# Logits of gathered tree rows on VectorE: sixteen multiply-and-sum instructions per tile in place of one multiply, one reduction and one addition

## The reference, cut to what matters

```python
xn = _layernorm(x, axis=-1)                      # 16 x 256 tokens, 128 features
logits = xn @ W_in.T + b_in                      # 4 trees, 1365 nodes each, 4 logits a node
act4 = gelu(logits).reshape(B, 4, 1365, 4)
decisions = argmax(act4, axis=-1)
current = 0
for d in range(5):
    current = next node at level d + 1, by the decision at the current node
masked = act4 * (one-hot of the 6 nodes on the path)
g = silu(masked.reshape(B, -1) @ W_out.T)
x = x + s * g                                    # s: output of a gated recurrence over xn
```

## Time and profile before

| what | us |
|---|---|
| median of 3 runs (lowest to highest) | 1540.62 (1540.55 to 1541.93) |
| the profiled execution, its own time | 1541.28 |
| its span, first to last instruction | 1538.6 |
| busy: PE, DVE, ACT, POOL | 1294.0, 1297.0, 1232.8, 1007.1 |
| mean granted TensorE clock, 1 is 2.4 GHz | 0.938 |
| L750: 64 instructions, busy | 147.7 |
| L751: 64 instructions, busy | 146.3 |
| L754: 64 instructions, busy | 19.0 |

### The profile page before, as it was taken

The page is one execution under the profiler, slowest core; times in us unless marked ns, Lnnn a source line. Parts: engine busy times, 40 slices in busy tenths (PEclk is TensorE's granted clock), DMA queues, the critical chain, the costliest instruction groups (busy, mean ns, idle before and its releaser), DMA issues. The chain is left out here.

```text
span 1538.6 us, 29520 instructions
## 1 busy us (share of the span) xinstructions
PE 1294.0 (84%) x9368; PEld 882.8 (57%) x9368; DVE 1297.0 (84%) x2503; ACT 1232.8 (80%) x3433; POOL 1007.1 (65%) x1471
## 2 busy tenths in 40 slices
PE   5997888888887566992699999999999999999976
PEld 3665656666666342441466666666666666666654
DVE  2388898989989983686899999999999999999943
ACT  2368887989879875772698998998989999999964
POOL 0257677685777850476877877778777777787712
PEclk9999899999999677996999999999999999999988
DMA  4268777687777961896010111101111111111005
GB/s 112 100 216 294 273 274 284 210 309 262 272 277 241 362 217 42 258 297 224 22 33 23 44 45 35 43 12 44 44 44 34 27 29 45 44 34 44 9 12 168
DMA packets 148010, 206.00 MB, mean 134 GB/s; under 512 B 67984, under 2 KB 101136, under 8 KB 147728
## 3 DMA queue, kind: packets, MB, share of 16 engines
q0 software_dynamic: 36864, 134.76, 25.1%
q1 hardware_dynamic: 110560, 67.78, 16.0%
q10 hardware_dynamic: 432, 1.59, 0.3%
HBM read 166.87 MB, written 24.64 MB: 124 GB/s over the span
## 5 line engine op out<-in xcount | busy, mean ns | idle before, releaser
L335 POOL DMA_INDIRECT l_rows<-in_table,l_idx x256 | 315.1, 1231 | 200.9 <-DVE l_idx L795 107.2
L640 ACT ACTIVATE l_rows<-l_rows,l_act 128x128 f32<-128x128 f32 x1024 | 306.3, 387 | 2.1
L1572 ACT ACTIVATE lo_s_ps<-lo_s_ps,lo_nmx,lo_rn 128x128 f32<-128x128 f32 x512 | 222.8, 440 | 1.9 <-DVE lo_nmx L1830 1.5
L474 PE MATMUL l_acc<-ident,l_rows 128*128 128x128 f32 x1024 | 159.6, 306 | 47.2 <-ACT l_rows L640 45.9
L474 PEld LDWEIGHTS l_acc<-ident,l_rows 128*128 128x128 f32 x1024 | 128.2, 156 | 81.2 <-ACT l_rows L640 73.3
L750 DVE TENSOR_TENSOR l_rows<-l_rows,xn_tok 128x2048 f32<-128x2048 f32 x64 | 147.7, 2307 | 8.8 <-DMA l_rows<-in_table,l_idx 8.8
L440 PE MATMUL l_S<-pre,l_AT 128*128 128x144 f32 (+3 forms) x832 | 129.9, 308 | 28.1 <-ACT l_AT L631 28.1
L440 PEld LDWEIGHTS l_S<-pre,l_AT 128*128 128x128 f32 (+2 forms) x832 | 117.0, 207 | 58.2 <-ACT l_AT L631 42.5
L751 DVE TENSOR_REDUCE l_dot<-l_rows 128x16 f32<-128x2048 f32 x64 | 146.3, 2286 | 2.2
L1708 POOL TENSOR_TENSOR lo_de_kS<-lo_de_S,lo_de_ops 128x384 f32<-128x384 f32 x128 | 127.9, 999 | 10.0
L1726 POOL TENSOR_TENSOR lo_c<-lo_c,lo_rn 128x512 f32<-128x512 f32 x64 | 66.8, 1043 | 98.9 <-ACT lo_rn L1621 96.3
(11 more groups left out here) (267 smaller groups left out, 3483.3 us busy)
## 6 DMA issues: line engine op xcount, KB each, us to landing
lo_VE<-lo_V SPq DMA_DIRECT2D x64, 128.0 KB, 2.9
scratch_ops<-prepared_then_rounds SPq DMA_DIRECT2D x4, 1792.0 KB, 6.7
lo_de_ops<-scratch_ops SPq DMA_DIRECT2D x16, 448.0 KB, 4.4
l_rows<-in_table,l_idx POOLq DMA_INDIRECT x256, 6.0
scratch_qo<-prepared_then_rounds SPq DMA_DIRECT2D x8, 512.0 KB, 8.2
lo_de_qo<-scratch_qo SPq DMA_DIRECT2D x16, 256.0 KB, 4.7
x_tok<-in_x SPq DMA_DIRECT2D x8, 256.0 KB, 5.3
scratch_x<-x_tok SPq DMA_DIRECT2D x8, 256.0 KB, 10.7
```

The costliest lines, as they stand in the source:

```text
L335: pool.indirect_dma_start(rows[L][:, r % SLOTS, p, :], None, a[f"table{L}"], bass.IndirectOffsetOnAxis(ap=at[:, p:p + 1], axis=0)).then_in ...
L474: ins = pe.matmul(out, rows[L][:, r % SLOTS, p, (FAN + f) * D:(FAN + f + 1) * D], m["ident"][:], start=False, stop=(L == 5 and k == PICK - ...
L640: ins = act.activation(z, z, ACT.Copy, scale=actv[L][:, r % 2, k:k + 1])
L1572: ins = act.activation(here, here, ACT.Exp, scale=rn[:, v % 2, j, 2 * k + e:2 * k + e + 1], bias=nmx[:, j, e, k:k + 1], accum_out=sums[:, ...
```

## The change

`dots` computes each of the 16 logits by an instruction of its own, `tensor_tensor_reduce`. It multiplies 128 gathered weights by the token's 128 features in place, and adds up the products, starting from the bias (a per-partition scalar, read from the gathered row), into one column of `pick`. The buffer `dot`, the two waits of DVE on itself and the addition of the biases are gone. The wait on `act_ready` of tile r - 2 now stands ahead of all of it. The last instruction of the 16 signals ACT.

```diff
-        dot = {L: sb(f"l0_dot{L}", [P, PICK]) for L in (4, 5)}
...
-                prod = rows[L][:, s, :, 0:FAN * D].rearrange("p t (f d) -> p t f d", d=D)
-                x = m["xn_tok"][:, r, :].unsqueeze(1).unsqueeze(1).broadcast_to([P, TREES, FAN, D])
-                ch.link(dve.tensor_tensor(prod, prod, x, ALU.mult))
-                ch.link(dve.tensor_reduce(four(dot[L][:]), prod, AX.X, ALU.add))
                 if r >= 2:
                     dve.wait_ge(act_ready[L].sem, act_ready[L].after(r - 2))
-                dve.tensor_tensor(four(pick[L][:, r % 2, :]), four(dot[L][:]), rows[L][:, s, :, 2 * FAN * D:], ALU.add).then_inc(pick_ready[L].sem, 1)
+                x = m["xn_tok"][:, r, :]
+                for k in range(PICK):
+                    row = rows[L][:, s, k // FAN, :]
+                    z, bias = row[:, k % FAN * D:(k % FAN + 1) * D], row[:, 2 * FAN * D + k % FAN:2 * FAN * D + k % FAN + 1]
+                    ins = dve.tensor_tensor_reduce(z, z, x, 1.0, bias, ALU.mult, ALU.add, accum_out=pick[L][:, r % 2, k:k + 1])
+                ins.then_inc(pick_ready[L].sem, 1)
```

## The result

The changed kernel is faster. Over 17 runs of each its median is 1529.51 us (1523.87 to 1536.99) against 1540.58, a ratio of 0.9931 with a 95% interval of 0.9918 to 0.9944: 11 us less. The profiled execution took 1530.51 us, with a span of 1528.7.

A forecast was written before the change was run, and what follows sets the result against it. DVE was taken to bound the phase, with ACT close behind. The profiled 1541.3 us plus 35 for the calls and 15 for the shared port gave 1591, range 1540 to 1705; the likeliest case's own range was 1550 to 1642.

The forecast's parts named there:

- What bounds the phase: All `dots` calls but the first: DVE is the bound, busy 450 of 496 us, with ACT 8 us a round behind.
- A call before: One `dots` call in the kernel before: 4.89 us from L750, L751 and L754, so 313 us for 64 calls.
- the write of the sum: Second, 128 x 1 instruction after each main one on DVE: 0.08 us, from BN_AGGR and ACT's accumulator read.
- The main instruction: DVE's 128 x 128 multiply-and-sum for each logit: a step of 0.195 us, from BN_STATS, plus 0.06 for its bias.
- the scalar: Bias read as a per-partition scalar by each main instruction: 0.06 us more a step, from L1856 against L1807.
- a summing form: ACT's summing activation steps 0.35 us against 0.30 plain; a trace let in, rounding the pair from 0.335 to 0.34.
- The shared port: POOL and two-SBUF-input DVE instructions shut each other out, now for nearly the whole `dots` call: +15 us, bounds 0 and 41.
- The first rival: A main instruction plus write costs 0.29 us or less, turning point 0.291; at 0.265 the kernel takes 1514 us; chance 0.11.
- ACT's overlap: ACT's main and accumulator read overlap, 0.44 us from main to main, not 0.64; at 0.44 on DVE, 1694 us.
- The half rate: The skill's rule slows the summing form with two SBUF sources: 0.475 us with its write, 1729 us; chance 0.08.
- POOL was not starved: Third rival: DVE never yields the port within a call, a round takes 84 us instead of 64, 1701 us; chance 0.06.
- The moved wait: `act_ready` wait of tile r - 2, placed 4.6 us earlier on DVE: costs nothing, since DVE waits for ACT nowhere.

The follow-up runs named there:

- the constant seed: Changed kernel with the 16 biases left out, each sum starting from constant 0 instead of a per-partition scalar: 1511.4 us, ratio 0.9802 to the kernel before.

## Why the prediction was wrong

- **What bounds the phase** was right: DVE. Of 12.5 us that the calls lost, 10.3 came through. That something close behind DVE limits a larger gain was right too, but not where: I let at most some 60 us of saved DVE time through. With the constant seed the calls take 69 us less than before (312.7 to 243.4) and 31 reach the end, and no run gained more than some 33. Busy sums alone did not show that.
- **A call before**, 4.89 us and 313 for 64, was right: the timeline gives 312.7.
- **The step that failed is the write of the sum, 0.08 us a pair.** I took it from BN_AGGR's step and from ACT's read of its accumulator. On DVE it measures 0.010. Over 1024 pairs the error is 72 us, more than the whole distance of 62 between forecast and result; the other terms erred the other way.
- **The main instruction** was near: 0.195 for 128 elements and 0.06 for the scalar give 0.255, measured 0.263 without the write. The scalar's 0.06 was exact. The 0.008 that is left is close to the 0.005 that I let in for a summing form. The two have not been measured apart from each other.
- **The shared port** was right as a mechanism and short by over a quarter: +15 us predicted, 20.6 of standstill measured. But I had DVE wait for most of POOL's four elementwise instructions a round, and nearly all of the loss is at two of them, the scaling and the shift; the two halvings of the gates cost 1.5 us in all.
- **The first rival, faster, was the case that came**, and its turning point of 0.291 us a pair was worked out rightly; at 0.273 its own formula gives (4.37 - 4.89) x 64 + 15 = -18, and with the port's 20.6 it is -13. I gave it 0.11 because I held ACT's overlap for the closest pattern. The half rate had nothing to it, and POOL was not starved: its gathers got shorter.
- **The moved wait** costs nothing, as said, within 0.5%.

## What to carry to other kernels

Price a row of short instructions by the step from start to start, and never by the sum of their durations: here the durations said +74 us and the steps -33. Before replacing an instruction with one SBUF input by one with two, see what POOL does meanwhile, and move POOL's elementwise work if it falls into that time; the same move can lose where the port is mostly free. A per-partition scalar in a short instruction is worth taking out, when one wide instruction can do its work afterwards.

## What the runs showed of the hardware that was not expected

- DVE's read of its accumulator, recorded with 0.08 us, starts with the next main instruction and adds 0.010 us to a pair (0.273 against 0.263). ACT's steps 0.09.
- `tensor_tensor_reduce` with two f32 inputs in SBUF takes 1.03 ns an element, on a fixed part of some 0.14 us with a scalar (0.207 less 64 x 0.00103) and 0.08 without (0.213 less 0.132), by two lengths.
- POOL and DVE take turns by the instruction: in a row of sixteen, one of DVE's gets done between two of POOL's. It lasted 1.88 us and the next one 1.40, beside two of POOL of 1.28 and 1.26. POOL's indirect DMAs hold DVE up hardly at all: 623 steps beside them have a mean of 0.274 us and a longest of 0.35.
